# An attention and feed-forward kernel on one core: maxima and exponentials over pairs of PSUM banks, causal masks by matmul, and the maxima sent in two transfers a half

## The reference

```python
h = _layernorm(x, axis=-1) * (1 + ca) + sa
x = x + ga * attention(h)          # causal, 16 heads
h = _layernorm(x, axis=-1) * (1 + cb) + sb
x = x + gb * ffn(h)                # token shift, three 256x256 products

def attention(inputs):
    scores = jnp.einsum('bhqd,bhkd->bhqk', q, k) * Hd ** (-0.5)
    scores = jnp.where(causal, -jnp.inf, scores)
    attn = jax.nn.softmax(scores, axis=-1)
    return jnp.einsum('bhqk,bhkd->bhqd', attn, v)
```

## Time and profile before

| | |
|---|---|
| median of 3 runs | 1524.66 us (1518.13 to 1531.08) |
| the profiled execution's own time | 1521.95 us |
| its span, first to last instruction | 1520.0 us, 28003 instructions |
| mean granted TensorE clock | 0.927 of 2.4 GHz |

### The profile page before, as it was taken

How to read it: one execution, slowest core, us unless ns; L and a number is a source line. 1 busy time by engine, 2 the same in 40 slices (tenths; PEclk the granted TensorE clock), 3 DMA queues, 4 the chain that set the end, 5 groups by cost and what they waited for, 6 DMA issues and landing times.

```text
span 1520.0 us, 28003 instructions
## 1 busy us (share of the span) xinstructions
PE 1346.2 (89%) x8744; PEld 746.3 (49%) x8744; DVE 1118.0 (74%) x3435; ACT 958.2 (63%) x1916; POOL 678.7 (45%) x1098
## 2 busy tenths in 40 slices
PE   5898889899998999889998899989998999998855
PEld 4443434455554555444554455545454555544444
DVE  8778667877678777877678777787778777777234
ACT  2167556766677666676677566776667666666633
POOL 4014122554436354553446545364546534343554
PEclk9598979999899999999899999999999898999878
DMA  4321124122331224222242223312232222221100
GB/s 139 75 64 47 42 50 112 49 65 68 84 86 46 54 66 118 67 54 55 67 108 53 56 70 97 82 44 54 72 105 63 64 54 76 68 58 50 38 29 28
DMA packets 90005, 101.77 MB, mean 67 GB/s; under 512 B 29681, under 2 KB 55545, under 8 KB 89857
## 3 DMA queue, kind: packets, MB, share of 16 engines
q1 hardware_dynamic: 89280, 99.20, 25.0%
q10 hardware_dynamic: 576, 0.79, 0.3%
HBM read 30.69 MB, written 8.94 MB: 26 GB/s over the span
## 4 chain that ended last, share of the span: by engine, by line
PE 51%; DVE 13%; SPq 10%; ACT 9%; issue 8%; POOL 7%; DMA 2%; ACTq 0%; POOLq 0%; DVEq 0%
PE val_ps L1286 13%; PE col_ps L1235 12%; PE row_ps L1264 9%; SPq L493 6%; ACT weights L815 5%; DVE row_ps L1035 5%; PE dense_ps L1296 4%; SPq L505 3%; PE dense_ps L1298 3%; PE dense_ps L1297 3%; PE dense_ps L1324 2%; DVE max_parts L1039 2%; POOL weights L664 2%; PE dense_ps L1339 2%; ACT xn_c L859 1%
## 5 line engine op out<-in xcount | busy, mean ns | idle before, releaser
L815 ACT ACTIVATE weights<-col_ps 128x512 f32<-128x512 f32 (+2 forms) x1280 | 643.7, 557 | 319.9 <-PE col_ps L1235 305.2
L1035 DVE CUSTOM_DVE_ANT_0 row_ps<-row_ps,row_mask 128x128 f32<-128x128 f32 (+3 forms) x1024 | 477.4, 517 | 209.7 <-PE row_ps L1264 209.3
L1235 PE MATMUL col_ps<-q_stack,k_stack 64*128 64x512 f32 (+3 forms) x1536 | 400.9, 410 | 36.1 <-ACT weights L815 20.4
L664 POOL TENSOR_SCALAR_AFFINE_SELECT weights<-weights 128x256 f32<-128x256 f32 x512 | 211.0, 425 | 460.1 <-ACT weights L815 458.7
L1039 DVE TENSOR_REDUCE max_parts<-row_ps 128x1 f32<-128x512 f32 x512 | 328.7, 681 | 86.5 <-PE row_ps L1264 84.8
L1286 PE MATMUL val_ps<-weights,v_ones 128*32 128x512 f32 (+3 forms) x3072 | 349.9, 529 | 25.6 <-POOL weights L664 18.1
L1264 PE MATMUL row_ps<-k_stack,q_stack 62*128 62x512 f32 (+3 forms) x1536 | 341.6, 434 | 29.3 <-DVE max_parts L1039 11.8
L1235 PEld LDWEIGHTS col_ps<-q_stack,k_stack 64*128 64x128 f32 x1536 | 210.5, 196 | 224.7 <-ACT weights L815 174.4
L1264 PEld LDWEIGHTS row_ps<-k_stack,q_stack 62*128 62x128 f32 x1536 | 163.8, 197 | 242.2 <-DVE max_parts L1035 79.9
L1035 DVE DVE_READ_ACCUMULATOR2_ANT max_parts<- 128x1 f32 x1024 | 144.7, 141 | 0.0
L1286 PEld LDWEIGHTS val_ps<-weights,v_ones 128*32 128x32 f32 x3072 | 62.1, 110 | 117.8 <-issue 61.6
(11 more groups left out here) (194 smaller groups left out, 1893.8 us busy)
## 6 DMA issues: line engine op xcount, KB each, us to landing
q_stack<-q_part SPq DMA_DIRECT2D x384, 64.0 KB, 2.2
k_stack<-k_part SPq DMA_DIRECT2D x372, 64.0 KB, 2.2
xa<-in_x SPq DMA_DIRECT2D x8, 1024.0 KB, 5.6
q_stack<-max_rows SPq DMA_DIRECT2D x512, 2.0 KB
att<-val_out SPq DMA_DIRECT2D x64, 128.0 KB
recips<-recip_rows SPq DMA_DIRECT2D x32, 256.0 KB
xq<-in_x SPq DMA_DIRECT2D x28, 256.0 KB, 3.3
out<-xq SPq DMA_DIRECT2D x28, 256.0 KB, 2.1
```

The costliest lines, as they stand in the source:

```text
L664: nc.gpsimd.affine_select(out=w, in_=w, compare_op=ALU.is_ge, fill=0.0, base=0, pattern=[[0, 2], [1, P]], channel_multiplier=-1).then_inc( ...
L815: nc.scalar.activation(weights[:, t % 2, heads[0]:heads[-1] + 1:2, 0:q1 - q0], col_ps[bank][:, 0:n * (q1 - q0)].rearrange("p (h q) -> p h ...
L1035: last = nc.vector.tensor_tensor_reduce(out=scores, in0=scores, in1=row_mask[:, HALF - width:HALF], scale=1.0, scalar=MASKED, op0=ALU.add, ...
L1235: last = nc.tensor.matmul(col_ps[bank][:, i * (q1 - q0):(i + 1) * (q1 - q0)], stack_at(k_stack[s % 2], rows, heads[i], P * j, P * (j + 1)) ...
```

## The change

1. `row_ps` and `col_ps` become tensors of two adjacent banks. `maximum` reduces both banks of a pair in one `reduce_max`; `exps` takes both banks of a column pair in one activation. The semaphores are raised by 2 at the end of it, so the refill of either bank waits for both.
2. The mask is no longer added by DVE. For each diagonal block PE adds it in PSUM by matmuls in bf16 from two constants (`mask_ident`, a shifted identity, and `mask_fill`, 0 or -3e38), in two steps of 64 partitions each: 128 columns, then the last 64 columns. Even and odd heads again lie on two halves of the array's rows. That is 16 blocks a group of heads, 512 in all, of four matmuls each. Every pair is then a plain reduction.
3. The turn of the maxima is four transposes of 32x32 onto 32 partitions instead of one of 128x32, and `place_max` issues 2 DMAs a half instead of 8.
4. DVE takes both units of the early pair at once, ahead of the emptying of the dense bank.

```diff
-PLACED = 2 * (P // SQUARE) * 16
+PLACED = 2 * 16
...
-        col_ps = [ps(f"col_ps{i}", [P, HALF]) for i in range(COL_BANKS)]
-        row_ps = [ps(f"row_ps{i}", [P, HALF]) for i in range(ROW_BANKS)]
+        col_pair = ps("col_ps", [P, COL_BANKS, HALF])
+        row_pair_ps = [ps(f"row_ps{i}", [P, 2, HALF]) for i in range(ROW_BANKS // 2)]
+        col_ps = [col_pair[:, i, :] for i in range(COL_BANKS)]
...
-        max_rows = [sb(f"max_rows{i}", [P, 2 * MROWS * 8]) for i in range(2)]
+        max_rows = [sb(f"max_rows{i}", [SQUARE, P]) for i in range(2)]
...
                     row = ROW_TILE * odd + MAX_AT
-                    rows = stack[row:row + MROWS, half].rearrange("p g n -> p (g n)").bitcast(F32).rearrange(
-                        "p (r q n) -> p r q n", q=P // SQUARE, n=SQUARE)
-                    for q in range(P // SQUARE):
-                        lo = SQUARE * q + 8 * MROWS * odd
-                        sp.dma_start(rows[:, :, q, :], max_rows[half][lo:lo + 8 * MROWS, :]
-                                     ).then_inc(max_placed[half], 16)
+                    sp.dma_start(stack[row:row + MROWS, half].rearrange("p g n -> p (g n)").bitcast(F32),
+                                 max_rows[half][8 * MROWS * odd:8 * MROWS * (odd + 1), :]).then_inc(max_placed[half], 16)
...
-            nc.gpsimd.affine_select(out=row_mask[:, HALF - P:HALF], in_=row_mask[:, HALF - P:HALF], compare_op=ALU.is_ge,
-                                    fill=MASKED, base=0, pattern=[[-1, P]], channel_multiplier=1
-                                    ).then_inc(consts_done, 1)
-            pool.wait_ge(consts_done, 2)
+            for odd in range(2):
+                pool.wait_ge(consts_done, odd + 1)
+                rows = slice(ROW_TILE * odd, ROW_TILE * (odd + 1))
+                nc.gpsimd.affine_select(out=mask_ident[rows], in_=mask_ident[rows], compare_op=ALU.not_equal, fill=1.0,
+                                        base=0, pattern=[[ROW_TILE, 2], [-1, P]], channel_multiplier=1)
+                nc.gpsimd.affine_select(out=mask_fill[rows], in_=mask_fill[rows], compare_op=ALU.is_ge,
+                                        fill=MASKED, base=0, pattern=[[ROW_TILE, 2], [-1, P]],
+                                        channel_multiplier=1).then_inc(consts_done, 1)
+            pool.wait_ge(consts_done, 3)
 
...
                 n = len(heads)
-                act.wait_ge(cols_ready, exp_index(b, s, c) + 1)
+                act.wait_ge(cols_ready, exp_index(b, s, c) + 2)
                 if c == COL_FIRST[t]:
 
                     wait(act, val_done, val_index(b, s, t) - 1)
-                bank, _ = bank_of(COLS * s + c, COLS * G, COL_BANKS)
-                nc.scalar.activation(weights[:, t % 2, heads[0]:heads[-1] + 1:2, 0:q1 - q0],
-                                     col_ps[bank][:, 0:n * (q1 - q0)].rearrange("p (h q) -> p h q", h=n),
-                                     ACT.Exp, scale=SCALE).then_inc(exp_done, 1)
+                nc.scalar.activation(weights[:, t % 2, heads[0]:heads[0] + 2 * n, 0:q1 - q0].rearrange(
+                    "p (n o) q -> p o n q", o=2), col_pair[:, :, 0:n * (q1 - q0)].rearrange(
+                    "p o (n q) -> p o n q", n=n), ACT.Exp, scale=SCALE).then_inc(exp_done, 2)
...
-                    for c in units[:2]:
+                    for c in units[:1]:
                         exps(b, s, t, c)
                     for item in at:
                         between(*item)
                     normalise_next(b, kind, s, t)
-                    for c in units[2:]:
+                    for c in units[2::2]:
                         exps(b, s, t, c)
...
                 at = unit_index(b, s, u)
-                bank = row_ps[bank_of(UNITS * ((s + 1) % G) + u, UNITS * G, ROW_BANKS)[0]]
-                dve.wait_ge(rows_ready, at + 1)
+                banks = row_pair_ps[bank_of(UNITS * ((s + 1) % G) + u, UNITS * G, ROW_BANKS)[0] // 2]
+                dve.wait_ge(rows_ready, at + 2)
                 i, heads, k0, k1, second = ROW_UNITS[u]
-                half, odd = i // 4, heads[0] % 2
-                col = (SPANS_AT + 16 * second + 8 * odd if half else WHOLE_AT + 16 * odd) + 4 * (heads[0] // 2) + i % 4
-                dest = max_parts[half][:, col:col + 4 * len(heads) - 3:4].bitcast(F32)
-                width = k1 - k0
-                if k1 == P * (i + 1):
-
-                    for n in range(len(heads)):
-                        scores = bank[:, n * width:(n + 1) * width]
-                        last = nc.vector.tensor_tensor_reduce(
-                            out=scores, in0=scores, in1=row_mask[:, HALF - width:HALF], scale=1.0, scalar=MASKED,
-                            op0=ALU.add, op1=ALU.max, accum_out=dest[:, n:n + 1])
-                else:
-                    last = nc.vector.reduce_max(dest, bank[:, 0:len(heads) * width].rearrange(
-                        "p (h k) -> p h k", h=len(heads)), AX_X)
-                last.then_inc(max_done, 1)
-                if u == FIRST_HALF - 1:
-                    split_max(b, s, 0, at + 1)
-                if u == UNITS - 1:
-                    split_max(b, s, 1, at + 1)
+                half, n = i // 4, len(heads)
+                apart = 8 if half else 16
+                col = (SPANS_AT + 16 * second if half else WHOLE_AT) + 4 * (heads[0] // 2) + i % 4
+                dest = max_parts[half][:, col:col + 2 * apart].bitcast(F32).rearrange(
+                    "p (o c) -> p o c", o=2)[:, :, 0:4 * n - 3:4]
+                nc.vector.reduce_max(dest, banks[:, :, 0:n * (k1 - k0)].rearrange("p o (n k) -> p o n k", n=n), AX_X
+                                     ).then_inc(max_done, 2)
+                if u == FIRST_HALF - 2:
+                    split_max(b, s, 0, at + 2)
+                if u == UNITS - 2:
+                    split_max(b, s, 1, at + 2)
...
                 wait(dve, max_placed[half], (b * G + (s + 1)) * PLACED)
-                nc.vector.transpose(max_rows[half][:], parts[:, 0:SQUARE].bitcast(F32)).then_inc(max_turned, 1)
+                for q in range(P // SQUARE):
+                    cols = slice(SQUARE * q, SQUARE * (q + 1))
+                    last = nc.vector.transpose(max_rows[half][:, cols], parts[cols, 0:SQUARE].bitcast(F32))
+                last.then_inc(max_turned, 1)
...
                         empty_dense(*item)
-                    for u in early[1:]:
-                        maximum(b, s, u)
                     for item in at:
                         mix(*item)
-                    for u in late:
+                    for u in late[::2]:
...
                 for n in range(len(pair[0])):
                     for odd, heads in enumerate(pair):
                         if n == 0:
                             banks[odd] = row_bank(b, s, u + odd)
                         rows = slice(ROW_TILE * odd, ROW_TILE * odd + MAX_AT)
-                        end = n == len(heads) - 1
+                        end = n == len(heads) - 1 and not diagonal
                         last = nc.tensor.matmul(banks[odd][:, n * width:(n + 1) * width],
                                                 stack_at(q_stack[stack], rows, heads[n], P * i, P * (i + 1)),
                                                 stack_at(k_stack[stack], rows, heads[n], k0, k1),
                                                 start=(n == 0), stop=end, skip_group_check=True)
                         if end:
                             last.then_inc(rows_ready, 1)
+                for n in range(len(pair[0])) if diagonal else ():
+                    for a in range(2):
+                        for odd in range(2):
+                            rows = slice(ROW_TILE * odd, ROW_TILE * (odd + 1))
+                            end = n == len(pair[0]) - 1 and a == 1
+                            last = nc.tensor.matmul(banks[odd][:, (n + 1) * width - P + ROW_TILE * a:(n + 1) * width],
+                                                    mask_ident[rows, a, :], mask_fill[rows, a, ROW_TILE * a:P],
+                                                    start=False, stop=end, skip_group_check=True)
+                            if end:
+                                last.then_inc(rows_ready, 1)
 
```

10 lines of the change are left out of this document (7 added, 3 removed).

## The result

| | before | after |
|---|---|---|
| median (4 runs each) | 1522.78 us | 1568.71 us (1559.47 to 1572.16) |
| ratio | 1 | 1.029, 95% interval 1.022 to 1.035 |
| the profiled execution's own time | 1521.95 us | 1572.16 us |
| mean granted TensorE clock | 0.927 | 0.939 |

A forecast was written before the change was run, and what follows sets the result against it. PE was taken to bound the kernel, busy for 1346 of 1520 us. The terms, 54 - 30 - 13 - 12 + 12 + 3 - 5 = +9 us on 1521.95 us, gave 1531 us; range 1470 to 1580.

The forecast's parts named there:

- Exponentials: ACT's operations over column pairs: -12 us from earlier ends, +12 us (5 to 20) from broken overlap with PE's refill.
- Rival B: The column pair starves ACT, PE and ACT taking turns on one pair of banks: 51 us, 1570 us; chance 0.10.
- rival A: Masks on PE go at the pace of weight loads, 0.22 us a block: 95 us, 1572 us; chance 0.17.
- Masks: Mask matmuls on PE: 0.15 us a block, 77 us in all, of which +54 us (31 to 95) on the path.
- the lower bound: Least price of a mask block on PE: 128 + 64 columns with loads hidden, 0.087 us.
- Maxima: Row maxima on DVE: about 80 us of DVE time saved, giving PE -30 us (-15 to -45); order put at nothing.
- Transfers: DMAs of the maxima, two issues for eight: PE's wait for them goes, -13 us (-10 to -14).
- the 4 us: How much earlier the maxima land with two DMA issues instead of eight; said to cover the longer turn.
- Selects: POOL's selects in steps with one pair: first starts up to 0.5 us later, +3 us (0 to 20).
- Clock: Granted PE clock: fewer waits for DVE, some more for ACT, -5 us (-15 to +10).

The follow-up runs named there:

- e3: Kernel before with only the turn and transfers changed (four 32x32 transposes, two transfers a half): 1540.63 us, ratio 1.0067.
- e7: e1 with one plain reduction a bank, in the old DVE order (early unit, dense emptying, second early unit): 1544.70 us, ratio 1.0105.
- e10: e7 with both units of the early pair ahead of the emptying of the dense bank: 1519.70 us, ratio 0.9907.
- e1: Kernel after with single exponentials, each waiting for and releasing its own bank: 1517.13 us, ratio 0.9899 to the kernel before.
- e2: Kernel before with only the exponentials taken over a pair of banks: 1560.93 us, ratio 1.0199.
- e4: e1 without the 2048 mask matmuls, so the causal mask of the maxima is left out: 1496.15 us, ratio 0.9777.
- e12: Kernel before with only both units of the early pair moved ahead of the emptying of the dense bank: ratio 0.9937.
- e5: e1 with joint start: the first of two single exponentials waits for both banks, each releases its own: 1572.3 us, ratio 1.0261.
- e6: e1 with joint release: PE refills either bank only after both single exponentials: 1555.54 us, ratio 1.0156.
- e8: e1 with pair maxima kept, but the early pair's maximum moved behind the emptying of the dense bank: 1542.59 us, ratio 1.0087.

## Why the prediction was right or wrong

A path from before to after, one edit at a time, by the ratios: turn and transfers +0.7% (e3), masks to PE with plain reductions in the old order +0.4% (e7), both early units ahead -2.0% (e10), one operation for two -0.1% (e1), exponentials over the pair +3.9% (after). In microseconds of 1525: +10, +6, -30, -1, +59; together +44. Steps of under 0.7% are at the edge of what the intervals tell apart. The last step is 52 us by the times of e1 and after, and e2 shows that it depends on what else is there (+30 us on the kernel before). Set side by side start by start, the two profiled executions of e1 and after differ by 28 us where both run at the full clock and by 24 us where just one does; for before and e2 it is 22 and 12. So what the pair costs by its waits is much the same in both, and the rest is clock.

**Exponentials: this is the step that failed.** The gain and the loss were put at 12 us each, the loss on the ground that the broken overlap costs 0.25 us once a group, 32 times, "with a few more places". In sum nothing was forecast, and 52 to 59 us came. The mechanism was named rightly, but its size wasn't: some 230 places, not 32, at 0.40 us. The sentence that hid it was "In the middle of a step PE has a microsecond of values in between and the second refill ended that wait before, so nothing changes": 175 of the 234 close pairs stand in the middle of a step. It looked only at PE. ACT's next start depends on the refill too, and it had been starting 0.26 us behind its last exponential because the first bank was filled early. Rival B put the price at a third of 386 pairs and 0.4 us, 51 us in all, 1570 us; the price a place was right, the places were 230 rather than 129, and the shorter operation gave ACT 45 us back. It was the right rival, with a chance of 0.10 that was too small: the earlier trace rows showed four exponentials on end, and the count of pairs that close together could have been taken from the trace. That its 1570 us, and rival A's 1572, lie so close to the 1568.71 us is in part chance, since their sums have the masks at 54 and 95 us. The rule of the Trainium skill (Trainium Kernel Development and Optimization, Best Practices) to double-buffer, which the page gives for overlapping DMA with compute, would have spoken for this rival if carried over to banks; the trace agrees with that, with 259.6 us of waits of PE's loader for exponentials, and 171.6 us when the two banks take turns again (e1).

**Masks.** Forecast 0.15 us a block, measured 0.09, the lower bound; that is 46 us instead of 77, and the price is where the term was wrong. The share on the path was right: 31 us at equal full clock (e4, e1) are 0.7 of the 46. In the time 21 us came instead of 54, since the clock gave some back. Rival A falls, since bf16 loads don't set the pace here: a block takes no longer than its columns by the lower bound, 0.087 us. The loader's mean is 99 ns for a mask and 193 ns for a row score. The Trainium skill (TensorE: Matmul & The Clock Gate, Weight-path perf modes) has such loads of types other than FP32 in a faster mode; by the estimate drawn from it a block takes 0.11 us, and the trace, with 0.09, agrees in direction and is lower still.

```profile
L1262 PEld LDWEIGHTS row_ps<-k_stack,q_stack 62*128 62x128 f32 x1536 | 143.3, 193 | 220.7 <-issue 129.5
...
L1273 PEld LDWEIGHTS row_ps<-mask_fill,mask_ident 64*128 64x128 bf16 x2048 | 57.7, 99 | 40.3 <-issue 25.2
```

**Maxima.** -30 us was forecast, mainly for shorter operations. That the emptying of `xq` no longer stands between a pair's two units was named as a further gain without a number, and what the order costs was put at nothing. The runs have it the other way round: the order -30 us, the operation over two banks -1. That the order by itself gives the number of the forecast is chance. The masked operations' part isn't separate: e7 less e3, masks on PE and plain reductions together, is +6 us, not told apart from nothing; less the 21 us of the masks, an estimate of -15 for the plain reductions would be left.

**Transfers.** -13 us was forecast; -10 on e1, at the edge of the noise, and +10 on the kernel before. The step that failed there is "The longer turn, up to 0.6 us, is covered by the 4 us": that covers the transfers' path, not what is queued behind the turn on DVE.

**Selects.** +3 us was forecast; the loader's wait for them went from 48.6 to 41.9 us. Nothing to be seen, as expected.

**Clock.** -5 us was forecast. By the line above 0.939 against 0.927, the clocks of the two profiled executions, would be -9; side by side, with the mask matmuls counted to the steps that they stand in, before and after differ by -8 us where just one runs at the full clock. The term is larger than I thought where it matters most: e1 is 15 us faster than before at a clock 0.043 higher, which would be 33 us if the line, whose runs end at 0.931, went on that far. Side by side e1 takes 34 us more than before where both run at the full clock, about the price of the masks, and 34 us less where just one does. So without its exponentials the change gains by the clock, and by nothing else that these traces show.

**The version that beats both** is e1: the change without its exponentials, 1517.13 us, 1.0% (0.5 to 1.5) under the kernel before and 3.8% under the kernel after by the ratios. e10 equals it; e12 has 0.6% with one moved line.

## What to carry to other kernels

Two banks that are filled and read one by one are a double buffer, even where they look like a pair; one operation over both makes them a single one, and saving 0.07 us a pair cost 0.40 us wherever the next pair stood close behind. Before merging two operations, count in the trace how often the consumer starts the next one sooner than the producer's refill takes, and look at both sides of the buffer. Look at PE's busy time of the same instructions as well as at its idle time: a reordering that moves a long stand away can pay in clock alone. Where two kernels have the same matmuls, set their starts side by side and sort them by the granted clock: that parts what was waited for from what went with the clock.

## What the runs showed of the hardware that was not expected

- A transpose of 32x32 takes 200 ns and one of 128x32 takes 212 ns: four small ones cost four times as much, 51 us for 13.5 in the kernel.
- Mask matmuls in bf16, two side by side with a load each, take 0.09 us for a step of 128 columns and one of 64 together; one step of two float32 matmuls of 128 columns took 0.11 us.
- An exponential over two banks takes 1023 ns and two overlapping ones 1.08 to 1.09 us, yet pairs behind it begin at the least 0.61 us after it, against 0.52 us behind two single ones with a joint start (e5) or release (e6). Where the 0.09 us come from stays open.
- The idle time of PE was equal in e1 and e8, and their times differed by 25 us: stretches that only one of them ran at 1.2 GHz took it about 1.5 times as long.
